# Sorted edge rows of 576 bytes in place of 520, in a graph-layer kernel on one core

## The reference

```python
h   = maximum(layernorm(x), 0)
in_deg  = minimum(segment_sum(ones, dst), 511)
out_deg = minimum(segment_sum(ones, src), 511)
sum3d   = segment_sum(edge_attr @ W_sum + b_sum, src)      # 212,500 edges -> 12,500 nodes
out = x + h + z_in[in_deg] + z_out[out_deg] \
        + sigmoid(cent @ W_cent + b_cent) + sigmoid(vor @ W_vor + b_vor) + sum3d
```

## Time and profile before

| what | value |
|---|---|
| time, median of 3 executions | 2479.94 us (2478.37 to 2482.51) |
| span of the profiled execution | 3079.2 us |
| TensorE's mean granted clock in it | 0.703 of full speed |
| busy: POOL / DVE / PE / ACT | 60% / 55% / 53% / 27% |
| DMA traffic in it | 451.89 MB, 147 GB/s on average |

### The profile page before, as it was taken

The page is one execution under the profiler, slowest core; times in us unless marked ns, Lnnn a source line. Parts: engine busy times, 40 slices in busy tenths (PEclk is TensorE's granted clock), DMA queues, the critical chain, the costliest instruction groups (busy, mean ns, idle before and its releaser), DMA issues.

```text
span 3079.2 us, 40112 instructions
## 1 busy us (share of the span) xinstructions
PE 1621.7 (53%) x8689; PEld 1230.9 (40%) x8689; DVE 1683.0 (55%) x5737; ACT 819.8 (27%) x4073; POOL 1853.9 (60%) x1869
## 2 busy tenths in 40 slices
PE   5644555455555432226555554444456665568766
PEld 1223444344333320014444444333355554456655
DVE  7554456666666631346656654333455554468866
ACT  3312222232322332442232322222222222200323
POOL 5556665556565667665555655656655555556676
PEclk7756666666666655557767777767777777789988
DMA  4245433334444443334555555555556666579896
GB/s 122 85 127 151 116 106 107 99 104 122 122 121 121 126 135 106 88 107 137 155 152 164 160 160 161 143 151 148 155 156 181 183 187 178 169 189 231 210 248 187
DMA packets 485070, 451.89 MB, mean 147 GB/s; under 512 B 72407, under 2 KB 444637, under 8 KB 484828
## 3 DMA queue, kind: packets, MB, share of 16 engines
q1 hardware_dynamic: 402782, 300.08, 37.0%
q0 software_dynamic: 78752, 136.44, 14.1%
q10 hardware_dynamic: 3294, 12.80, 1.3%
HBM read 319.28 MB, written 129.59 MB: 146 GB/s over the span
## 4 chain that ended last, share of the span: by engine, by line
another core or an unknown queue 34%; DVE 19%; PE 17%; issue 15%; ACT 7%; DMA 3%; SPq 2%; POOL 2%; DVEq 1%; ACTq 0%; POOLq 0%
PE bank L1001 8%; ACT junk L864 6%; DVE hot_dh L605 3%; DVE hot_n L670 3%; DVE acc L697 2%; DVE hot_dl L605 2%; PE bank L949 2%; POOL sorted L513 2%; DMA edge_ring<-in_L_gnn_z_out_dram,out_i 2%; SPq L408 2%; DVE gate_normed L736 2%; PE bank L984 1%; PE bank L1026 1%; DVE hot_t L605 1%
## 5 line engine op out<-in xcount | busy, mean ns | idle before, releaser
L513 POOL DMA_INDIRECT sorted<-edge_ring,pos_i x1660 | 1605.8, 967 | 1103.1 <-DVE pos_i L799 633.4
L1001 PE MATMUL bank<-piece_ring,hot_n 128*125 128x129 f32 x4920 | 885.4, 336 | 260.0 <-DVE hot_n L670 209.0
L864 ACT ACTIVATE junk<-bank,mark_col 128x100 bf16<-128x100 f32 x1664 | 550.4, 343 | 1748.6 <-remote 1221.3
L1001 PEld LDWEIGHTS bank<-piece_ring,hot_n 128*125 128x125 f32 x4920 | 823.2, 241 | 367.0 <-DVE hot_n L670 248.7
L697 DVE TENSOR_TENSOR acc<-bank,acc 125x129 f32 x1230 | 352.8, 287 | 698.6 <-remote 523.9
L984 PE MATMUL bank<-hot_w,after_b 128*128 128x400 bf16 x416 | 189.3, 455 | 806.1 <-ACT junk L864 560.7
L670 DVE SCALAR_TENSOR_TENSOR hot_n<-bank,wkey,piece_ring 128x250 f32<-128x250 f32 x1230 | 579.9, 472 | 11.8 <-issue 5.2
L984 PEld LDWEIGHTS bank<-hot_w,after_b 128*128 128x128 bf16 x416 | 49.5, 119 | 866.8 <-ACT junk L864 594.3
L864 ACT ACTIVATION_READ_ACCUMULATOR junk<-bank,mark_col 128x1 f32 x1664 | 338.1, 203 | 12.3 <-issue 12.3
L605 DVE TENSOR_TENSOR hot_dl<-dst_parts,bank 128x400 bf16<-128x400 bf16 x416 | 148.0, 356 | 337.1 <-remote 305.5
L1026 PE MATMUL bank<-hot_dl,hot_dh 128*125 128x100 bf16 x1661 | 207.2, 276 | 237.4 <-DVE hot_dh L605 197.6
(11 more groups left out here) (109 smaller groups left out, 1183.2 us busy)
## 6 DMA issues: line engine op xcount, KB each, us to landing
piece_ring<-sorted SPq DMA_DIRECT2D x1230, 130.0 KB
edge_ring<-in_edge_attr_dram SPq DMA_DIRECT2D x332, 320.0 KB
sorted<-edge_ring,pos_i POOLq DMA_INDIRECT x1660
base<-in_x_dram SPq DMA_DIRECT2D x20, 560.0 KB
out_dram<-base ACTq DMA_DIRECT2D x19, 560.0 KB
out_dram<-base SPq DMA_DIRECT2D x9, 560.0 KB
base<-out_dram SPq DMA_DIRECT2D x9, 560.0 KB
edge_ring<-in_L_gnn_z_out_dram,out_i POOLq DMA_INDIRECT x100
```

The costliest lines, as they stand in the source:

```text
L513: g.indirect_dma_start(rows, bass.IndirectOffsetOnAxis(index, 0), edge_ring[:, slot, at, :], None).then_inc(s_scatter[slot], 16)
L864: last = a.activation(junk[:, t, :], part[:, t // 2, :, t % 2], ACT.Relu, bias=mark_col[:, :], accum_out=pos_f[:, q % 4, t:t + 1])
L1001: last = t_.matmul(to, hot_n[:, n % HOT_SLOTS, k, :], piece_ring[:, n % PIECE_SLOTS, k, 0:SUM], start=(k == 0), stop=(k == ROW_GROUPS[s] - 1))
```

## The change

A row of `sorted` gets 144 numbers (576 bytes) in place of 130 (520 bytes). The 14 numbers behind the key are filled with ones once, at the start, and never used. With the row grow `edge_ring`, each load of a piece (147,456 bytes in place of 133,120), each scatter (73,728 bytes in place of 66,560) and the row pitch in SBUF. The ring of pieces goes from twelve places to ten and that of one-hots from nine to eight. What is computed, summed or multiplied is the same.

```diff
-PIECE_SLOTS = 12
-HOT_SLOTS = 9
+PIECE_SLOTS = 10
+HOT_SLOTS = 8
...
-    ROW, SUM, KEY = F + 2, F + 1, F + 1
+    ROW, SUM, KEY = F + 16, F + 1, F + 1
...
-            v.memset(edge_ring[:, :, :, F:SUM], 1.0)
-            v.memset(edge_last[:, F:SUM], 1.0)
+            v.memset(edge_ring[:, :, :, F:ROW], 1.0)
+            v.memset(edge_last[:, F:ROW], 1.0)
...
-                                       in1=piece_ring[:, n % PIECE_SLOTS, 0:G, KEY:ROW].to_broadcast([P, G, LOC]),
+                                       in1=piece_ring[:, n % PIECE_SLOTS, 0:G, KEY:KEY + 1].to_broadcast([P, G, LOC]),
...
-                    a.activation(edge_last[:, KEY:ROW], key_f[:, FULL:NT], ACT.Copy).then_inc(s_row_key, 1)
+                    a.activation(edge_last[:, KEY:KEY + 1], key_f[:, FULL:NT], ACT.Copy).then_inc(s_row_key, 1)
```

## The result

The change makes the kernel slower by a third of a percent: 2488.01 us (median of 6, 2485.16 to 2494.22) against 2478.58 us for the kernel before (median of 6, 2476.42 to 2482.51), a ratio of 1.0034 with a 95% interval of 1.0021 to 1.0047. That is 8.4 us by the ratio, between 5 and 12. The forecast was 2482 us, range 2469 to 2491, with "same" as the likeliest sign.

What follows compares the result with a forecast made beforehand. The prediction took POOL's scatters to bound the loop, and DVE, then POOL, the tail. Its terms summed to 2 us, all from longer piece loads; added to 2479.9 they gave 2482 us, range 2469 to 2491 us.

Steps and rivals of the forecast that it cites:

- the weak point that the prediction had named: Loop: timed runs keep POOL's pace, inferred from one sum: 3079.2 - 590 = 2489 us, near the 2479.9 median.
- Longer scatters, 0 us: In the loop: 1660 scatters of longer rows take no longer; 0 us, bounds 0 and 11 us.
- The rival of cut packets: In the loop: each scatter is cut in two packets, 0.24 us each, 400 us in all, 2880 us; chance 0.03.
- Longer pieces in the tail, 2 us: In the tail, first stage DVE-bound, second POOL-bound: longer piece loads cost 2 us, bounds 0 and 9 us.
- The rival that DMA becomes the bound of the tail: In the tail: DMA bounds both stages, 6 to 9 us slower, up to 2489 us; chance 0.16.
- 76 to 79%: Tail's first stage: DMA queue 1's share of the engines with 110 pieces in 80 us; fewer pieces mean DMA bounds.
- The smaller rings, 0 us: In loop and tail: ten piece places, cycle 6.2 us where 7.3 are allowed, and eight one-hots cost 0 us.
- below 10 us of waits for pieces: Profile after: DVE's one-hots wait under 10 us for pieces; a starved ring would show tens of us.
- The fills at the start, 0 us: At the start: the longer fill takes about 0.5 us, while DVE waits 1.43 us for the first load; 0 us.
- The rival that wide rows pay: In the tail: aligned rows make transfers cheaper, 5 to 17 us faster, 2463 to 2475 us; chance 0.20.
- the share of the scatters' queue in a stretch of the loop: In the loop: up by 10.8% if rows cost by the byte, flat or lower if alignment pays.
- the forecast that POOL's pace hides everything: Whole kernel: 2482 us, chance 0.55; wrong if the timed executions differ by more than 5 us.

Runs made afterwards that it cites:

- e1: The kernel before, unchanged, profiled a second time: span 2488.4 us, its own time 2490.15 us.
- e10: e3 with 576-byte rows in the first three segments and 520 in the last, same as e7, on a fast chip: 2479.24 us, ratio 0.9991 to before.
- e8: e3 with 520-byte rows in all four segments, edge_ring still at 576 from row to row: ratio 0.9997 to before, which took 3073.18 us there.
- e7: e3 with 576-byte rows in the first three segments and 520 in the last: ratio 0.9994 to before, which took 3073.18 us there.
- e6: e3 with 576-byte rows in the last segment only, 520 in the others: ratio 0.9996 to before, which took 3073.18 us there.
- e9: e3 with 576-byte rows in the last segment only, same as e6, on a fast chip: 2487.47 us, ratio 1.0024 to before.
- e12: e9 with 608-byte rows in the last segment and six one-hots in place of eight: ratio 1.0044 to before, which took 3026.74 us there.
- e2: The kernel before, 520-byte rows, with only the rings cut to ten piece places and eight one-hots: 2481.86 us, ratio 0.9999 to before.
- e4: The changed kernel with twelve piece places in place of ten and six one-hots in place of eight: 2488.86 us, ratio 1.0031 to before.
- e5: The kernel before plus two more fills, of 400 and 80 numbers, at the start: ratio 1.0003 to before, which took 3073.18 us there.
- e11: e5 again on another chip: ratio 0.9998 to before, which took 3026.74 us there.
- e3: The changed kernel with edge_ring's long fill moved behind the fill that lets ACT issue its small loads: 2487.45 us, ratio 1.0019 to before.

## Why the prediction was right or wrong, point by point

**What bounds.** That the timed execution runs its loop at POOL's pace is right: in e1 the scatters take from 21.6 to 2140 us with 38.0 us of waits. The reason given, the weak point that the prediction had named, was wrong. The waits of the earlier trace rows were laid to the profiled execution, from one sum that came out within 0.4%; they belong to the kind of chip, and timed executions there are as long. That the sum hit 2489 us, against 2488.4 in e1, is in part luck. It took 590 us out of the loop; from that profile to e1 the time up to the last scatter falls by only 572.3 us (2712.4 to 2140.1), and the tail, which was left as it stood, falls by 18.5 (366.8 to 348.3). What makes those events late stays open.

**Longer scatters, 0 us.** Right: e10, with wide rows in three segments, is not slower. The medians of 958 and 962 ns occur with rows of either width (e8 has 958, e7 962, on the same chip) and with the same program (e6 and e9), so they are no price of the row; they are 6.6 us over 1660 scatters, though, about the spread of the times. The rival of cut packets didn't occur at 576 bytes: the packets of queue 0 are 78752 before and after. In e12, where it did occur, POOL's median stays at 958 ns, and at 960 over the 417 scatters from 2000 us on, 300 of which are cut; the 0.24 us that the rival put on each would have been seen.

**Longer pieces in the tail, 2 us.** This term was mis-sized: 5.9 us (3.7 to 8.2) by e9, inside the bounds of 0 and 9. The step that failed is the choice between them: "POOL keeps its pace in the stretch with 106%" argued from the second stage, where it is true, and the loss came in the first. There the shares had been added to 102% of what the engines could do, from a profile in which they stood at 0.90 to 0.95. On the chips that count they stand at 1.06 to 1.09 before the change (e10, e2, e1). The rival that DMA becomes the bound of the tail is what happened, in its first stage alone, where DMA already sets the pace before the change. That its price, 6 to 9 us, comes near the 5.9 is luck. It took 6.2 us from 80 us of the stage, by the bytes. Worked out the same way for the stage as timed, an estimate, the bytes would cost 0.77 x 0.108 x 133 = 11 us; the pieces came only 4.2% slower, and so it was about 5. The 3.1 us of the second stage didn't show. The sign that the prediction had named did: 77.4% for queue 1, inside its 76 to 79%, and fewer pieces, 143 in place of 147 in 120 us.

**The smaller rings, 0 us.** Right by e2. The argument that pieces are hardly waited for the earlier trace rows was not: on the fast kind of chip DVE waits 470.7 us for them, behind edge loads that POOL holds back. The cover was POOL's pace, as the text also said. So the sign "below 10 us of waits for pieces" failed, with either kernel. One number of the working was off as well: with twelve places and narrow rows its own terms leave 3.0 us to spare (8.7 - 5.7), not 2.5.

**The fills at the start, 0 us.** Wrong, by 1.4 us as the rows show it. Their length was right (0.46 us), and that DVE waits long enough after them was, too. The step that was left out is who waits for the fills: ACT issues its small load of `src` only after the last of them, and that load is now issued at 2.07 us, behind SP's load of `dst` (1.69 us), where it went out at 1.56 us, ahead of it. (The recorded expectation speaks of edge traffic; the order of the issues points to the load of `dst`. Which of the two delays the landing wasn't tested apart.) In ten profiles with ACT's load at 1.55 to 1.60 us the key step starts between 5.93 and 6.52 us; in four with 2.07 or 2.08 us (the changed kernel, e4, e5, e11) between 7.37 and 7.98. The first scatter comes 1.4 us later on average (23.4 in place of 22.0 us). That the start is later is shown in rows, also without wide rows. That the end is later by as much is argued, since POOL doesn't catch up in the loop; in time only e3 speaks for it, with overlapping intervals.

**Alignment.** The rival that wide rows pay did not win. What there is of it: from e1 to the changed kernel queue 1 moved 5.9% more bytes with 1.5% less engine time (45.7% of 2488.4 us against 45.1% of 2483.9), and the scatters' queue 8.7% more with 6%. The sign that the prediction had named, the share of the scatters' queue in a stretch of the loop, speaks against a gain there: from 1900 to 2000 us it rises from 14.4% (e1) to 16.2%, by 12.5%, for 10.6% more bytes. By the estimate from the Trainium skill, page "DMA: Bandwidth & Descriptors", section "How a descriptor splits into AXI transactions", pieces would cost 7% more and not 10.8%. The 4.2% of the tail's first stage is nearer to that than to 10.8%, and below both. The trace doesn't separate better starts from a price that each packet has whatever its length, nor from a better place in SBUF, whose pitch changed as well. In the loop none of it reached the time; in the tail it can only have made the loss smaller.

**The sum.** 5.9 + 1.4 = 7.3 us, against 8.4 (5 to 12) measured. The time lies in the range, and the likeliest sign was missed by the two terms together: each alone is near or below what can be measured. By the prediction's own test, wrong if the timed executions differ by more than 5 us, the forecast that POOL's pace hides everything failed.

No version beats both kernels clearly. e10 has the lowest time, 0.09% below before with an interval that ends at 0.9999, less than the 0.2% that I had said can be told from nothing.

## What to carry to other kernels

A wider row is paid where the transfer engines are full, and nowhere else: here 18% of the edges carried all of the cost, so look for the one stage with a DMA share above 1 and price the change there alone. The ratio of the bytes was too high a price for it: here 10.8% more bytes made the pieces 4.2% slower. When an instruction gets longer, ask not only whether its own engine has time but which semaphore stands behind it and whose DMA that lets go. And before a wait is explained away, check that the profile and the timed runs are of the same kind: a span a quarter above the time is a warning, not a rounding.

## What the runs showed of the hardware that was not expected

The same program takes 2480 us on some chips and 3027 to 3073 us on others, with a mean granted clock of 0.76 to 0.77 and 0.70 to 0.72 in their profiles. On the latter ACT waits 1191 to 1287 us for events that the profile can't place; by the kernel's code they are the ranks that PE makes. In those jobs a change of 0.3% could hardly be measured: the intervals were 0.2% wide to either side.

The DMA share of one core's 16 engines reached 1.06 to 1.09 over 120 us, at 238 to 249 GB/s. The traffic grew with the length of the pieces at the same share, so 239 GB/s was not yet all that it could be.

A delay of 0.5 us in issuing a load of a few bytes put off its first use by about 1.5 us, and in each such profile SP's much larger load of `dst`, issued at about 1.7 us, went out ahead of the small load and not behind it. That this order is the cause is argued from the rows, not shown by a run of its own.
